# Attention and expert layer on one core: weighted sums behind the shift, key parts on ScalarE, routing later

## The reference, cut to what matters

```python
def _L0_attn_ref(x, qkv_w, proj_w, proj_b):          # H 16 heads of 8, blocks of BS 64 rows, M 8 blocks
    q, k, v = (qkv[0], qkv[1], qkv[2])
    qb = q.reshape(B, H, M, BS, HD).mean(axis=3)
    kb = k.reshape(B, H, M, BS, HD).mean(axis=3)
    c = jnp.einsum('bhmd,bhnd->bhmn', qb, kb) * SCALE
    thresh = jax.lax.top_k(c, k_keep)[0][..., -1:]   # k_keep is 1
    block_mask = (c >= thresh) | jnp.eye(M, dtype=bool)
    ...
    probs = jax.nn.softmax(scores, axis=-1)
    out = jnp.einsum('bhqk,bhkd->bhqd', probs, v)
    return out @ proj_w.T + proj_b

def _L0_ffn_ref(x, w1, b1, w2, b2, wr, br):          # 4 experts of 512, the best 2 per row
    topk_vals, topk_idx = jax.lax.top_k(logits, K)
    gates = jax.nn.softmax(topk_vals, axis=-1)
    h = jax.nn.gelu(jnp.einsum('nd,edh->enh', xf, w1) + b1[:, None, :], approximate=False)
    y = jnp.einsum('enh,ehd->end', h, w2) + b2[:, None, :]
    ...
x = x + _L0_attn_ref(_layernorm(x), ...)
x = x + _L0_ffn_ref(_layernorm(x), ...)
```

## Time and profile before

| | |
|---|---|
| median of 3 runs | 947.48 us (944.78 to 947.55) |
| the profiled execution | 949.11 us, its span 947.50 us |
| granted TensorE clock, mean | 0.987 of full speed |
| TensorE matmuls busy | 868.6 us, 92% of the span |
| VectorE busy | 551.5 us, 58% |
| ScalarE busy | 455.2 us, 48% |
| GpSimd busy | 182.3 us, 19% |
| chain that ended last, by engine | TensorE 79%, ScalarE 7%, VectorE 6% |

### The profile page before, as it was taken

The page is one execution under the profiler, slowest core; times in us unless marked ns, Lnnn a source line. Parts: engine busy times, 40 slices in busy tenths (PEclk is TensorE's granted clock), DMA queues, the critical chain, the costliest instruction groups (busy, mean ns, idle before and its releaser), DMA issues.

```text
span 947.5 us, 24244 instructions
## 1 busy us (share of the span) xinstructions
PE 868.6 (92%) x9638; PEld 580.4 (61%) x9638; DVE 551.5 (58%) x1554; ACT 455.2 (48%) x740; POOL 182.3 (19%) x183
## 2 busy tenths in 40 slices
PE   3696898999999999999999999999999999999995
PEld 2475675656656565665656566665656666566652
DVE  7456647475665747566574756657475665736321
ACT  1332473735446373644637364463736446374641
POOL 5601111213021121302112130311203031111211
PEclk9798999999999999999999999999999999999998
DMA  7350432516243250625335062533506253350110
GB/s 207 102 145 21 128 119 77 163 26 183 73 142 114 80 163 23 183 73 146 108 83 172 12 183 73 146 110 90 167 13 180 73 146 98 92 155 3 57 56 13
DMA packets 96022, 99.40 MB, mean 105 GB/s; under 512 B 8969, under 2 KB 82705, under 8 KB 95905
## 3 DMA queue, kind: packets, MB, share of 16 engines
q1 hardware_dynamic: 93168, 85.09, 32.0%
q0 software_dynamic: 2544, 12.58, 4.2%
q10 hardware_dynamic: 192, 0.13, 0.1%
HBM read 48.10 MB, written 28.71 MB: 81 GB/s over the span
## 4 chain that ended last, share of the span: by engine, by line
PE 79%; ACT 7%; DVE 6%; issue 4%; SPq 2%; DMA 2%; POOL 1%; POOLq 0%; another core or an unknown queue 0%; DVEq 0%; ACTq 0%
PE y_ps L403 22%; PE s_ps L310 10%; PE o_ps L346 7%; PE s_ps L259 6%; PE s_ps L261 5%; PE s_ps L260 5%; PE s_ps L335 4%; ACT hid L962 4%; PE o_ps L353 3%; PE v_ps L326 2%; PE v_ps L365 2%; PE a_ps L376 2%; PE v_ps L319 2%; SPq L1135 2%; PE a_ps L268 2%
## 5 line engine op out<-in xcount | busy, mean ns | idle before, releaser
L403 PE MATMUL y_ps<-hid,w2s 128*128 128x512 f32 x480 | 241.5, 599 | 0.0
L926 ACT ACTIVATE prob<-s_ps 128x1024 f32<-128x1024 f32 x128 | 131.2, 1025 | 213.3 <-PE s_ps L335 211.9
L663 DVE TRANSPOSE_TENSOR_REDUCE rmax<-s_ps 128x16 bf16<-128x512 f32 x256 | 168.8, 700 | 84.6 <-PE s_ps L310 83.1
L962 ACT ACTIVATE hid<-s_ps,b1s 128x512 f32<-128x512 f32 x256 | 171.2, 688 | 35.4 <-PE s_ps L261 34.9
L310 PE MATMUL s_ps<-qdiag,kv 64*128 64x512 f32 x768 | 132.7, 450 | 2.6 <-DMA qdiag<-qpair 1.9
L1062 POOL TENSOR_TENSOR yT<-yT,gate_cols 128x512 f32<-128x512 f32 x48 | 61.7, 1285 | 314.4 <-DVE gate_cols L759 314.0
L259 PE MATMUL s_ps<-xnhi,w1hi 128*128 128x512 f32 x256 | 111.4, 435 | 1.5
L919 ACT COPY vaug<-v_ps 128x128 f32<-128x128 f32 x128 | 34.0, 266 | 162.0 <-PE v_ps L319 155.3
L672 DVE TENSOR_REDUCE nmax<-v_ps 128x64 bf16<-128x256 bf16 x128 | 54.1, 423 | 87.4 <-PE v_ps L326 87.3
L310 PEld LDWEIGHTS s_ps<-qdiag,kv 64*128 64x128 f32 x768 | 84.8, 252 | 29.1 <-ACT hid L962 10.6
L261 PE MATMUL s_ps<-xnhi,w1lo 128*128 128x512 f32 x256 | 100.9, 394 | 0.0
(11 more groups left out here) (149 smaller groups left out, 1076.6 us busy)
## 6 DMA issues: line engine op xcount, KB each, us to landing
gate_cols<-gates SPq DMA_DIRECT2D x64, 256.0 KB, 4.0
kv_table<-stage SPq DMA_DIRECT2D x16, 768.0 KB, 3.9
kv<-stage SPq DMA_DIRECT2D x16, 768.0 KB
kv_chosen<-selected SPq DMA_DIRECT2D x15, 768.0 KB, 5.1
kv<-kv_chosen SPq DMA_DIRECT2D x15, 768.0 KB, 4.9
qdiag<-qpair SPq DMA_DIRECT2D x504, 16.0 KB
xs<-in_x SPq DMA_DIRECT2D x16, 256.0 KB, 5.2
out_x<-x SPq DMA_DIRECT2D x16, 256.0 KB, 5.6
```

The source lines that it names most:

```text
L403: ins = pe.matmul(dst[:], w2s[:, n, :], hid[:, n, :], start=(c == 0), stop=(c == C - 1))
L663: v.tensor_reduce(rmax[m % 2][:, :, half * P // 2:half * P // 2 + HH].rearrange("p k h -> p h k"), s_ps[m % 2][:, half * N:(half + 1) * N] ...
L926: act.activation(prob[m % 2][:].rearrange("p h s -> p (h s)"), s_ps[m % 2][:], ACT.Exp, scale=SCALE).then_inc(exped, 1)
L962: act.activation(hid[:, k, :], up_ps[up_bank(k)], ACT.Gelu, bias=b1s[:, k:k + 1]).then_inc(gelued, 1)
```

## The change

Six things, all in the order of the work:

1. On TensorE `weighted(m-1)` stands behind `shift(m)` for all batches; `o_rows` comes behind the second `c_down` of a block.
2. ScalarE takes the exponential ahead of `o_copy`, and the copies of xn's high part, of k's high part and of v ahead of the copy of the values.
3. The cast of k to its high part moves from VectorE to ScalarE (`a_k_high`, signalled by `k_high`), for batches from 2 on; VectorE keeps the block sum and the low part (`a_k_low`).
4. The block products move from the end of block 4 to block 5 on TensorE, and `a_qk` from block 4 to the end of `a_k_low`, in block 3, on VectorE.
5. `c_logits` moves from block 1 to block 6 on VectorE, its exponential from block 2 to 7 on ScalarE, `c_gates` from block 4 to 7 on VectorE, the transpose of the gates from block 6 to the seventh up-projection, its copy behind `c_rows`.
6. `a_select` scales and masks in one instruction in place of two.

```diff
@@ stages @@
-            return (2, 0, 1, 3) if b == 0 else (2, 3, 4, 4)
+            return (2, 0, 1, 3) if b == 0 else (2, 3, 4, 5)
@@ TensorE @@
+                ahead = b >= 1 and b + 1 < B
                 for m in range(M):
-                    if m >= 1 and b >= 2:
-                        weighted(b, m - 1)
                     row_max(b, m)
-                    if m >= 1 and b < 2:
-                        weighted(b, m - 1)
...
                     shift(b, m)
+                    if m >= 1:
+                        weighted(b, m - 1)
...
+                    if ahead and m == stages(b)[3]:
+                        a_products(b + 1)
...
+                    if b >= 2:
+                        c_down(b - 2, 2 * m + 1)
                     if m in (2, 4, 6):
                         o_rows(b, (m - 2) // 2)
-                    if b >= 2:
-                        c_down(b - 2, 2 * m + 1)
                     if m + 1 < M:
                         values(b, m + 1)
...
-                    if b >= 1 and m == 6:
-                        c_gates(b - 1)
...
+                    if k == 6 and b >= 1:
+                        c_gates(b - 1)
@@ VectorE @@
+            def a_k_low(b):
+                st, kview = stage[b % 2], block_ap(a_ps[:])
+                v.wait_ge(k_high, b - 1)
+                total = step(v.tensor_reduce(ksum[:], kview, AXX, ALU.add))
+                v.tensor_tensor(st[:, :, :, 1], kview, st[:, :, :, 0].bitcast(F32), ALU.subtract).then_inc(bank_a.free, 1)
+                return total
...
-                v.tensor_scalar(crow[:].rearrange("p m n -> p (m n)"), a_ps[:, 0:M * M], 1.0 / (BS * BS), SCALE,
-                                ALU.mult, ALU.mult).then_inc(bank_a.free, 1)
+                v.scalar_tensor_tensor(crow[:].rearrange("p m n -> p (m n)"), a_ps[:, 0:M * M], SCALE / (BS * BS),
+                                       mine_of[:].rearrange("p m n -> p (m n)"), ALU.mult, ALU.mult).then_inc(bank_a.free, 1)
                 v.wait_ge(bank_a.free, bank_a.at["products", b])
-                v.wait_ge(dve_step, step(v.tensor_tensor(crow[:], crow[:], mine_of[:], ALU.mult)))
...
-                    if ahead and m == 4:
-                        a_qk(max(q_total, k_total))
...
-                    if b >= 1 and m == 1:
-                        ranked = c_logits(b - 1)
...
                     if ahead and m == 3:
-                        k_total = a_k(b + 1)
+                        k_total = a_k_low(b + 1)
+                        a_qk(max(q_total, k_total))
+                    if ahead and m == 5:
+                        tied = a_select(b + 1)
+                    if b >= 1 and m == 6:
+                        ranked = c_logits(b - 1)
+                        c_split(b - 1)
                     if m in (2, 4, 6):
                         o_rows(b, (m - 2) // 2)
-                    if ahead and m == 5:
-                        tied = a_select(b + 1)
-                    if b >= 1 and m == 4:
+                    if b >= 1 and m == 7:
                         c_gates(b - 1, ranked)
-                    if b >= 1 and m == 6:
-                        c_split(b - 1)
-                    if b >= 1 and m == 7:
-                        c_gates_turned(b - 1)
...
                 c_rows(b)
+                if b >= 1:
+                    c_gates_turned(b - 1)
@@ ScalarE @@
+            def a_k_high(b):
...
+                act.copy(stage[j][:, :, :, 0], block_ap(a_ps[:])).then_inc(k_high, 1)
...
+                    shift_exp(b, m)
                     if m in (2, 4, 6):
                         o_copy(b, (m - 2) // 2)
-                    shift_exp(b, m)
                     if b >= 1 and m == 0:
                         c_columns(b - 1)
+                    if b >= 1 and b + 1 < B and m == 1:
+                        a_columns(b + 1)
+                    if b >= 1 and b + 1 < B and m == stages(b)[1]:
+                        a_k_high(b + 1)
+                    if b >= 1 and b + 1 < B and m == stages(b)[2]:
+                        a_v(b + 1)
                     if m in (3, 5, 7):
                         o_columns(b, (m - 3) // 2)
                     if m + 1 < M:
                         values(b, m + 1)
-                    if b >= 1 and m == 2:
+                    if b >= 1 and m == 7:
                         c_logits(b - 1)
...
```

More of the change, by code:

```diff
@@ L202, in layer @@
             sem(n) for n in ("scored", "blockmaxed", "shifted", "exped", "weighted_done"))
-        o_copied, o_turned, att_done = sem("o_copied"), sem("o_turned"), sem("att_done")
+        o_copied, o_turned, att_done, k_high = sem("o_copied"), sem("o_turned"), sem("att_done"), sem("k_high")
         mean2_done, rstd2_done, xn2_done, split_hi, split_lo = (
@@ L486, in tensor @@
                         o_project(b, (m - 4) // 2)
-                    if b >= 1 and b + 1 < B and m in stages(b)[:3]:
+                    if ahead and m in stages(b)[:3]:
                         project(b + 1, "qkv"[stages(b).index(m)])
+                    if ahead and m == stages(b)[3]:
+                        a_products(b + 1)
                     if b >= 2 and not edge:
                         c_down(b - 2, 2 * m)
-                    if b >= 1 and b + 1 < B and m == 1:
+                    if ahead and m == 1:
                         a_columns(b + 1)
+                    if b >= 2:
+                        c_down(b - 2, 2 * m + 1)
                     if m in (2, 4, 6):
                         o_rows(b, (m - 2) // 2)
-                    if b >= 2:
-                        c_down(b - 2, 2 * m + 1)
                     if m + 1 < M:
@@ L500, in tensor @@
                         c_route(b - 1, (0, 1))
-                    if b + 1 < B:
-                        if b == 0 and m in stages(b)[:3]:
+                    if b == 0:
+                        if m in stages(b)[:3]:
                             project(b + 1, "qkv"[stages(b).index(m)])
@@ L505, in tensor @@
                             a_products(b + 1)
-                    if b == 0 and m >= 5:
-                        (bias_out, bias_sum, bias_columns)[m - 5]()
-                    if b >= 1 and m == 6:
-                        c_gates(b - 1)
+                        if m >= 5:
+                            (bias_out, bias_sum, bias_columns)[m - 5]()
                 weighted(b, M - 1)
@@ L912, in a_v @@
                 act.copy(stage[j][:, :, :, 2].bitcast(F32), block_ap(src[:])).then_inc(of.free, 1)
+            def a_k_high(b):
+                j = b % 2
+                act.wait_ge(bank_a.full, bank_a.at["k", b])
+                act.wait_ge(table_out[j], 16 * times(b - 2, 2))
+                act.wait_ge(own_in[j], 16 * times(b - 2, 2))
+                act.copy(stage[j][:, :, :, 0], block_ap(a_ps[:])).then_inc(k_high, 1)
             def values(b, m):
@@ L986, in scalar @@
                         values(b, m + 1)
-                    if b >= 1 and m == 2:
+                    if b >= 1 and m == 7:
                         c_logits(b - 1)
-                    if b + 1 < B:
-                        if b >= 1 and m == 1:
-                            a_columns(b + 1)
-                        if m == stages(b)[2]:
-                            a_v(b + 1)
+                    if b == 0 and m == stages(b)[2]:
+                        a_v(b + 1)
                 if b == 0:
```

## The result

The changed kernel takes 953.13 us (median of 5 runs, 950.54 to 954.23), the kernel before beside it on the same chip 947.48 us (944.78 to 947.82). The ratio is 1.0065 with a 95% interval of 1.0043 to 1.0087: slower by 0.65%. The forecast was 956.3 us, with a range of 944 to 965.

The account below looks back on a forecast made before the run. TensorE's own stream was taken to set the pace. Middle batches + 5.7, batch 15 + 3.1, batch 1 + 0.1 and batch 0 nothing made + 8.9 us; from the median 947.48 the forecast was 956.3 us, range 944 to 965.

Parts of the forecast that it names:

- The fourth rival: Whole kernel: the terms balance, vaug waits of 0.39 to 0.46 us or savings elsewhere; within 0.3% of 947.5; chance 0.20.
- The wait for vaug: Before the row maximum, blocks 2 to 7: TensorE waits for ScalarE's copy, 0.53 us six times, 3.18 us a batch.
- The first rival: Before the row maximum: the vaug wait is short, 0.38 us, giving 943.8 us in all; chance 0.15.
- What is removed: TensorE waits in blocks 2 (0.96 us), 3 (0.49), 4 (1.16) and 6 (0.24) go: 2.85 us a batch.
- The third rival: Block 2: the chain from xnhi is late and the 0.96 us wait returns, up to 12.5 us, 969 us; chance 0.08.
- qk beside GpSimd's sum: VectorE, block 3: qk no longer overlaps GpSimd's sum, 0.21 us instead of 1.20; block 4's shift waits 0.18 us.
- The second rival: Before block 4's shift: qk stays 1.20 us and VectorE becomes the bound, 0.99 us more in 14 batches, about 970; chance 0.07.
- The sum of a middle batch: Batches 2 to 14: + 3.18 + 0.18 - 0.07 - 2.85 = + 0.44 us each, + 5.7 over 13 batches.
- block 4, products ... 1.16 us over the 0.20 ... gone: Block 4: the products' 1.16 us wait for ScalarE's stage copy of v goes, as the copy comes earlier and products move.
- a middle batch of 55.5 us: Sign that the forecast is right: a middle batch takes 55.5 us; under 54.9 would show it wrong.
- the last batch's blocks 35 us: Sign that the forecast is right: the last batch's eight blocks, 31.79 us before, take 35 us.
- Batch 1: Has the vaug waits already; two att waits less, attT and vaug copies later behind ScalarE's new work: + 0.1 us.

Follow-up runs that it names:

- after: The changed kernel itself, with all six changes, against the kernel before: 953.13 us, ratio 1.0065.
- the version of the gated sums: Changed kernel with values ahead of second c_down, keys' high parts on VectorE, c_gated of blocks 1, 3, 5 behind the next block's nmax: 910.05 us.
- the last two versions: The version of the gated sums (keys' high parts on VectorE, 910.05 us) and the same with them on ScalarE (912.38 us).
- the last one: The version of the gated sums with the keys' high parts on ScalarE, as in the changed kernel: 912.38 us, ratio 0.9611.

## Why the prediction was right, and where its steps were off

The direction and the mechanism held, and the time is in the range: 953.13 us against 956.3. Of the 8.9 us forecast 5.6 came. The fourth rival, within 0.3% of the kernel before, falls too: the interval begins at 1.0043. That the total came out this near is in part luck, as the items on the middle batch and on batch 1 show.

- **The wait for vaug** was the step on which all hung. Forecast 0.53 us, six times in a middle batch, a list entry of some 35 us; measured 0.72 against 0.20 to the next start, so 0.52, and 38.8 us in the list. The first rival (0.38 us) falls. The experiments that took the wait away, by place (0.984) or by cover (0.9761), give back more than the whole loss. The list gained 36 us of such waits, where some 35 were forecast.
- **What is removed**: block 2 to 0.87 us, block 3, the products and block 6 all as forecast. The third rival falls.
- **qk beside GpSimd's sum**: forecast 0.21 us, measured 0.22, and the shift of block 4 waits 0.19 us where 0.18 was forecast (scores 539.64 to shift 540.70, 1.06 against 0.87). The second rival falls. The Trainium skill (SBUF — State Buffer, "Who interferes with whom") says that a VectorE instruction with two SBUF inputs contends with a GpSimd instruction that reads SBUF. The trace agrees: the median of this line is 1202 ns before, beside GpSimd's sum in batch 9, and 224 ns after, where the sum starts at 540.39, behind qk.
- **The sum of a middle batch** was off: + 0.44 forecast, + 0.03 measured, 5.3 us over 13 batches. By intervals between row maxima, forecast and measured: block 1 to 2 +0.53 and +0.50, 3 to 4 +0.53 and +0.49, 4 to 5 -0.82 and -0.85, 5 to 6 +0.90 and +0.73, 7 to 0 +0.69 and +0.60; the others agree within 0.02. The largest piece is the step "block 4, products ... 1.16 us over the 0.20 ... gone". Before, the start after the products came 0.37 us behind them (544.18 to 544.55):

```profile
544.55 0.65 PE L346 MATMUL o_ps<-prob,vaug 128*32 128x64 f32 x32
```

  In block 5 it comes 0.17 behind (547.68 to 547.85). The wait thus had cost 1.36, not 1.16: a part of its restart stood in the distance after the matmul that had waited. That is 0.20 of the 0.41; the rest lies in pieces of 0.02 to 0.09, too small to give a cause. The signs "a middle batch of 55.5 us" and "the last batch's blocks 35 us" were missed by as much: 55.10, and 34.6 with the weighted sums that left the window.
- **Batch 1** was mis-sized: "+ 0.1" was forecast, +4.7 came. Length times clock stayed (51.5 and 51.1 us), so in the profiled execution it is the granted clock, which this step had left out although the clock in batch 1 was 0.94 already. There it made up for most of the error in the middle, and the start, 3.7 us shorter for a reason outside the change, went the other way. How much of the 4.7 us belongs to the kernel stays open. In the medians little room is left for it: the forecast less the 5.3 us of the middle is 951.0, and 953.13 came, so 2.1 us remain for the start and batches 0 and 1 together.
- **Batch 15**: + 3.1 forecast, +2.87 measured.
- **The parts**, each taken back alone. Against "after", in percent of the kernel before: the move of the weighted sums with its ScalarE order costs 2.6 (0.9809), the keys' high parts 0.45, the products' place 0.37; the routing's new place wins 0.23. My expectations had the weighted sums too large by 10 to 18 us each time. When the waits for vaug went, what is late next (oT, then att) took part of what I had counted as won; when they were added alone, one of them fell inside the wait of the products.

Open stays why the clock of batch 1 falls. Over one profile each, the five kernels with the key copy on VectorE have 54.7 to 57.4 us in batch 1 at clocks of 0.90 to 0.94, the nine with it on ScalarE 56.6 to 60.7 at 0.83 to 0.91. That this follows from the copy's place isn't shown. The mean clocks of all launches, which the middle batches with their 1.00 leave untouched, do not tell the two groups apart: 0.979 to 0.987 with the copy on VectorE, 0.980 to 0.986 on ScalarE. In the closest pair, the version of the gated sums, it is 0.979 on VectorE and 0.982 on ScalarE.

## What to carry to other kernels

When matmuls are moved, ask what they were covering: here 0.6 us of weighted sums covered a copy out of a shared PSUM bank, and moving them away cost 0.52 us at each of 84 places of this kernel, until other matmuls were put into the same gap (a move that won 3% over the changed kernel). Price a wait on a saturated engine by all starts around it, the one after the waiting instruction too. And when a wait is taken away, look up what is late next on the other engines before counting the whole of it as won.

## What the runs showed of the hardware that I had not expected

- The granted TensorE clock over batch 1 differs between profiles whose TensorE work there is the same: 0.94 (54.70 us), 0.86 (59.45), 0.83 (60.66). Launches of one kernel differ too: the kernel before, launched 23 times on one chip, took 944.41 us at a mean clock of 0.990 and 950.88 at 0.978. The batch's length follows it: length times clock lies between 50.3 and 52.7 us in the 13 kernels without added fillers. Of the levels 1.2 and 2.4 GHz such a mean is a mixture; within "after" the mean is 0.72 from 98 to 104 us and 1.00 from 104 to 110.
- The time to the first row maximum is 31.0 or 35.6 us in the last two versions, which have the same instructions there. The difference is one wait of ScalarE, for its first copy of the values. The timeline of ScalarE in the version of the gated sums:

```profile
35.22 0.27 ACT L935 COPY vaug<-v_ps 128x128 f32<-128x128 f32 x1 [6.68 <-remote]
```

  and in the last one:

```profile
30.08 0.27 ACT L935 COPY vaug<-v_ps 128x128 f32<-128x128 f32 x1 [1.39 <-PE v_ps L319]
```

  "Remote" stands where the profile finds no instruction of this core that released the wait. The kernel before had this wait too (5.92 us), the changed one had not, which is the -3.7 us of the first column; what is waited for isn't shown. Two single profiles shouldn't be compared by their spans below 0.5%, but by stretches.
- Two products of 64 columns cost TensorE 0.17 us in the stream, 0.37 behind a wait, and nothing inside another engine's copy.
